# Attention probabilities transposed by VectorE in 32x32 blocks and carried to their quadrants by small transfers, in place of TensorE's transposes

## The reference

```python
xn = _layernorm(x, axis=-1)
x = x + _L0_attn_ref(xn, ...) + _L0_ffn_ref(xn, ...)

# attention: 16 heads of 32, windows of W = 64 rows
qkv = xw @ qkv_w + qkv_b
attn = jnp.einsum('bnqhd,bnkhd->bnhqk', q, k) * scale
attn = attn + _rel_pos_bias(rel_bias, W)[None, None]
attn = jax.nn.softmax(attn, axis=-1)
out = jnp.einsum('bnhqk,bnkhd->bnqhd', attn, v)
return out @ proj_w + proj_b

# experts: each of 8 takes the 1024 rows with its highest scores
scores = (x_flat @ Wg.T).T
top_vals, token_idx = jax.lax.top_k(scores, capacity)
h = silu(xg @ W1.T) * (xg @ W3.T)        # per expert, written shorter here
y = (h @ W2.T) * softmax(top_vals)
out = zeros.at[token_idx].add(y)
```

## Time and profile before

| | |
|---|---|
| median of 3 runs | 2057.91 us (2055.49 to 2058.67) |
| the profiled execution | 2061.68 us |
| its span, first to last instruction | 2059.9 us |
| granted TensorE clock, mean | 0.991 |
| TensorE busy | 1999.6 us (97%) |
| VectorE busy | 1157.6 us (56%) |
| ScalarE busy | 663.1 us (32%) |
| GpSimd busy | 597.2 us (29%) |
| attention block / expert block | up to 983.8 us / the rest |

### The profile page before, as it was taken

One profiled execution on the slowest core, in us unless ns is written; L12 is line 12 of the kernel. 1 busy time (PEld: TensorE's weight loads), 2 busy tenths in 40 slices (PEclk: granted clock), 3 DMA queues, 4 the chain that ended last, 5 costly groups with the idle time before them and its releaser, 6 DMA issues.

```text
span 2059.9 us, 36125 instructions
## 1 busy us (share of the span) xinstructions
PE 1999.6 (97%) x15051; PEld 1619.1 (79%) x15051; DVE 1157.6 (56%) x1748; ACT 663.1 (32%) x1015; POOL 597.2 (29%) x416
## 2 busy tenths in 40 slices
PE   6999999999999999998899999999999999999997
PEld 4777777787778788776788888888888888888886
DVE  5666677777768877676744544346344443444221
ACT  2333322323334443332433242232332333323221
POOL 1444444445444343353022021211212012111111
PEclk9999999999999999999999999999999999999999
DMA  7133334555432111212444253333532434325311
GB/s 209 68 106 100 105 109 122 146 164 167 141 91 63 55 30 42 63 63 87 159 104 111 72 134 91 65 105 87 131 79 62 124 81 107 92 66 143 62 21 21
DMA packets 152883, 198.17 MB, mean 96 GB/s; under 512 B 19376, under 2 KB 93488, under 8 KB 152752
## 3 DMA queue, kind: packets, MB, share of 16 engines
q1 hardware_dynamic: 138416, 162.77, 26.3%
q0 software_dynamic: 14336, 33.56, 9.1%
HBM read 128.13 MB, written 51.38 MB: 87 GB/s over the span
## 4 chain that ended last, share of the span: by engine, by line
PE 52%; DVE 0%; POOL 0%; ACT 0%; issue 0%; POOLq 0%
PE ps_e L59 17%; PE ps_e L61 17%; PE ps_e L60 17%; PE ps_e L157 1%; POOL out_rows L1649 0%; DVE xn L1802 0%; DVE xgt_lo L1807 0%; ACT x_res L1717 0%; DVE w_lo L1796 0%; DVE got L165 0%; POOLq L1648 0%
## 5 line engine op out<-in xcount | busy, mean ns | idle before, releaser
L59 PE MATMUL ps_e<-xgt_hi,w_hi 128*128 128x512 f32 x1024 | 404.4, 395 | 7.7 <-DVE xgt_lo L1807 7.7
L61 PE MATMUL ps_e<-xgt_hi,w_lo 128*128 128x512 f32 x1024 | 399.3, 390 | 0.0
L60 PE MATMUL ps_e<-xgt_lo,w_hi 128*128 128x512 f32 x1024 | 399.2, 390 | 0.0
L1828 DVE TENSOR_TENSOR hm<-ps_e,silu 128x512 f32<-128x512 f32 x128 | 88.4, 691 | 458.5 <-PE ps_e L61 457.7
L59 PEld LDWEIGHTS ps_e<-xgt_hi,w_hi 128*128 128x128 f32 x1024 | 192.7, 188 | 46.0 <-DVE xgt_lo L1807 8.2
L1649 POOL DMA_INDIRECT out_rows<-x_res,idx x64 | 100.6, 1572 | 432.6 <-ACT x_res L1717 418.2
L61 PEld LDWEIGHTS ps_e<-xgt_hi,w_lo 128*128 128x128 f32 x1024 | 192.8, 188 | 40.7
L505 POOL TENSOR_TENSOR pn_sb<-p_sb,s_rec 128x1024 f32<-128x1024 f32 x64 | 121.9, 1904 | 350.0 <-DVE s_rec L1186 281.5
L60 PEld LDWEIGHTS ps_e<-xgt_lo,w_hi 128*128 128x128 f32 x1024 | 192.9, 188 | 38.2
L59 PE MATMUL ps<-xt_hi,wqk_hi 128*128 128x512 f32 x512 | 215.2, 420 | 3.2 <-issue 2.3
L186 POOL DMA_INDIRECT x_in<-xn_rows,idx x64 | 74.4, 1162 | 486.8 <-DVE idx L178 308.8
(11 more groups left out here) (182 smaller groups left out, 3489.1 us busy)
## 6 DMA issues: line engine op xcount, KB each, us to landing
x_f<-in_w SPq DMA_DIRECT2D x48, 512.0 KB
raw<-in_w SPq DMA_DIRECT2D x48, 512.0 KB
x_res<-in_x SPq DMA_DIRECT2D x16, 1024.0 KB, 5.3
out_rows<-x_res SPq DMA_DIRECT2D x16, 1024.0 KB, 4.2
xn<-x_in SPq DMA_DIRECT2D x256, 64.0 KB, 2.0
xn_rows<-xt_plain SPq DMA_DIRECT2D x10, 1024.0 KB, 4.2
xn<-xn_rows SPq DMA_DIRECT2D x32, 256.0 KB, 5.3
x_in<-xn_rows SPq DMA_DIRECT2D x28, 256.0 KB, 4.6
```

Of the source, the lines that this page charges most:

```text
L59: nc.tensor.matmul(out, w_hi, x_hi, start=start, stop=False)
L60: nc.tensor.matmul(out, w_hi, x_lo, start=False, stop=False)
L61: return nc.tensor.matmul(out, w_lo, x_hi, start=False, stop=stop)
L1828: v.tensor_tensor(hm[:, m % 2, :], ps[:, 2 * (m % 2) + 1, :], silu[:, m % 2, :], ALU.mult).then_inc(hm_ready, 1)
```

## The change

TensorE's transposes and `pt_diag` go, in all groups but the last two (62 and 63). GpSimd writes `pn_sb` in halves by key. VectorE transposes it in place in 32x32 blocks, one instruction of 1024 columns (`turn_probs`). Eight transfers of 32 partitions by 2 KB then carry the blocks to the quadrants in which the product wants them, into one of two buffers `pt` (`probs_piece`, `spread_probs`): four are issued by SyncE, four by ScalarE, each from its own queue, after a wait for `pn_turned` and for the product of the group two before. GpSimd's next multiply waits until the pieces of the group before have landed (`pt_in`), and so does the product.

The product is now one of 64 keys for one window at a time: 32 matmuls of 64 columns in place of 16 of 128, into two banks. V gets a second buffer. The eight PSUM banks are dealt out anew, with V's tiles and output tiles in banks of the scores and of Q and K, so their matmuls wait for other evictions than before. The orders of all queues are rewritten: V0 and V1 stand ahead of the scores of s, V2 and V3 ahead of those of s+1, the four output tiles around those of s+2, and each of the four products directly ahead of scores, while the bias add of the last group moves into the next chunk. The output rows' stored copy is waited for later by SyncE (`load_res`). Chunk 1's normalized rows are transposed by TensorE like those of chunk 0 (`first_xt`, `first_rows`), and both chunks' rows are stored by `keep_first`, 16 transfers each. The weight units come in another order, and V's evictions of chunk 0 stand between the splits.

The core of the diff:

```diff
+        pn_sb = sb("pn_sb", [P, TT * 4 * W])
+        pt = [sb(f"pt_{i}", [P, 2, TT, 4, QD]) for i in range(2)]
...
+        SP, OT, OT2, QB, KB = 0, 4, 5, 6, 7
+        V_BANK, P_BANK, FINAL_BANK = (0, QB, 0, QB), (0, 1, QB, KB), (0, 1, 2, 3)
...
+        def probs_piece(s, w, i, j):
+
+            half = TT * 4 * QD
+            src, dst = QD * (2 * w + i), QD * (2 * w + j)
+            return pt[s % 2][dst:dst + QD, i, :, :, :].rearrange("p t h q -> p (t h q)"), pn_sb[src:src + QD, half * j:half * (j + 1)]
...
+            def spread_probs(s):
+
+                sp.wait_ge(pn_turned, s + 1)
+                if s >= 2:
+                    sp.wait_ge(o_mm, s - 1)
+                for i, j in ((0, 0), (0, 1), (1, 0), (1, 1)):
+                    dst, src = probs_piece(s, 0, i, j)
+                    sp.dma_start(dst, src).then_inc(pt_in, 16)
...
+            keep_first(0)
             keep_scores(0)
+            keep_first(1)
+            spread_probs(0)
+            spread_probs(1)
+            keep_scores(1)
+            for c in range(1, NCH):
+                s, n, j = G * c, c + 1, c + LEAD
+                if n < FAR:
                     load_x(n)
...
+                spread_probs(s - 2)
+                load_res(c - 1)
                 if FAR < j <= NCH:
                     load_back_ahead(j - 1)
+                spread_probs(s - 1)
                 if n < FAR:
                     keep_xn(n)
+                    load_back(n)
+                spread_probs(s)
...
+            def normalise(s):
                 pool.wait_ge(rec_ready, s + 1)
...
+                    if s >= 1:
+                        pool.wait_ge(pt_in, PIECES * s)
+                    nc.gpsimd.tensor_tensor(halves_first(pn_sb[:, :]), p_sb[:, :, :, :].rearrange("p t h (j c) -> p (t h) j c", c=QD),
+                                            s_rec[:, :].unsqueeze(2).unsqueeze(3).to_broadcast([P, TT * 4, 2, QD]),
+                                            ALU.mult).then_inc(norm_ready, 1)
...
             def pv(s, m):
...
+                    pe.wait_ge(pt_in, PIECES * (s + 1))
...
+                    for w in range(2):
+                        keys = slice(W * w, W * (w + 1))
+                        for h in range(4):
+                            col = HD * (4 * m + h)
+                            i = nc.tensor.matmul(ps[HD * h:HD * (h + 1), (OT, OT2)[w], W * t:W * (t + 1)],
+                                                 v_rows[keys, t, col:col + HD], pt[s % 2][keys, :, t, h, :], start=True, stop=True)
...
+            def chunk(c):
...
                 project_q(s, 0)
                 project_k(s, 0)
+                project_v(c, 0)
+                hunt(c, 1)
+                project_v(c, 1)
+                pv(s - 2, 2)
+                pe.wait_ge(v_ready, TT * c + 1)
+                slot_read(c, 1)
                 scores(s)
+
+                pe.wait_ge(v_ready, TT * c + 2)
                 project_q(s + 1, 1)
+                hunt(c, 2)
                 project_k(s + 1, 1)
                 project_v(c, 2)
+                hunt(c, 3)
                 project_v(c, 3)
...
+                pe.wait_ge(v_ready, TT * c + 4)
+                project_q(s + 2, 2)
+                project_k(s + 2, 2)
+                hunt(c, 4)
...
+                hunt(c, 5)
+                lists_of(5)
+                project_out(c - 1, 2)
+                lists_of(6)
                 pv(s, 0)
...
+            def turn_probs(s):
+                dve.wait_ge(norm_ready, s + 1)
+                blocks = pn_sb[:, :].rearrange("p (b c) -> p b c", c=QD)
+                nc.vector.transpose(blocks, blocks).then_inc(pn_turned, 1)
```

More of the change, by code:

```diff
@@ L673, in hunt_chunk, with chunk @@
                 hunt(c, 5)
                 o_hi_part(s, 0, projected=TT * c)
+                exponentials(s + 2)
                 q_part(s + 3, 3)
[L677 to L680 removed]
                 k_part(s + 3, 3)
[L682 to L684 removed]
+            def chunk(c):
                 s = G * c
[L686 to L694 removed]
+                last = c == NCH - 1
+                o_hi_part(s - 3, 1)
+                spread_probs(s - 2)
@@ L715, in chunk @@
+                o_hi_part(s - 1, 3)
+                q_part(s + 2, 2)
+                exponentials(s + 1)
+                k_part(s + 2, 2)
+                if not last:
                     xt_hi_part(c + 1)
-                    k_part(s + 2, 2)
-                o_hi_part(s, 0, projected=None if first else TT * c)
+                spread_probs(s + 1)
+                o_hi_part(s, 0, projected=TT * c)
+                exponentials(s + 2)
                 q_part(s + 3, 3)
-                probs_t_part(s + 1)
@@ L735, in _ @@
             split_hi(1)
-            first_xt_hi()
-            for u in range(2, ALL_SPLIT):
-                split_hi(u)
+            split_hi(2)
             act.wait_ge(const_in, 96)
             nc.scalar.activation(q_bias[:, :], qk_bias[:, 0:G], ACT.Copy, scale=SCALE).then_inc(q_bias_ready, 1)
-            act.wait_ge(consts, 14)
             act.wait_ge(q_bias_ready, 1)
-            chunk(0, first=True)
+            q_part(0, 0)
+            split_hi(3)
+            k_part(0, 0)
+            split_hi(4)
@@ new lines, in chunk, with lists_of @@
+            def chunk(c):
+                s, n, j = G * c, c + 1, c + LEAD
+                ahead, last = FAR < j <= NCH, c == NCH - 1
+                def lists_of(g):
+                    if last:
+                        compact(nc, pe, lists, ps[:, LISTS, :], 0, g, parts=2)
+                project_q(s, 0)
+                project_k(s, 0)
+                project_v(c, 0)
+                hunt(c, 1)
+                project_v(c, 1)
+                pv(s - 2, 2)
+                pe.wait_ge(v_ready, TT * c + 1)
+                slot_read(c, 1)
@@ L1100, in last_chunk @@
                     project_out_group(t, 3).then_inc(p_mm, 1)
-            pe.wait_ge(consts, 14)
-            first_xt()
-            chunk(0, first=True)
-            for c in range(1, NCH - 1):
+            pe.wait_ge(consts, 12)
+            first_xt(0)
+            first_chunk()
+            for c in range(1, NCH):
                 chunk(c)
-            last_chunk()
+            last_rows()
         @block.vector
@@ L1211, in layernorm_apply_ahead @@
                     dve.wait_ge(gatef_mm, j - FAR)
-                for t in range(TT):
+                for t in tiles:
                     nc.vector.tensor_scalar(by_quadrant(xt_f[:, t, :]), by_tile(x_f[:, t, :]), mv_f[:, t, 0:1], rstd_f[:, t:t + 1],
@@ L1506, in last_chunk @@
[L1506 to L1515 removed]
+                v_part(c, 2)
+                turn_probs(s)
@@ L1535, in _ @@
             split_lo(0)
-            first_xt_lo()
-            for u in range(1, V_SPLIT):
-                split_lo(u)
+            first_xt_lo(0)
+            split_lo(1)
+            split_lo(2)
+            layernorm_stats(1)
             gate_rows(0)
-            for u in range(V_SPLIT, NO_PN_RAW):
-                split_lo(u)
-            layernorm_stats(1)
+            split_lo(3)
             layernorm_apply(1)
-            for u in range(NO_PN_RAW, ALL_SPLIT):
-                split_lo(u)
             dve.wait_ge(const_in, 96)
-            dve.wait_ge(consts, 14)
-            chunk(0, first=True)
+            dve.wait_ge(consts, 12)
+            v_part(0, 0)
+            split_lo(4)
+            v_part(0, 1)
+            split_lo(5)
+            add_bias(0, 0)
+            normaliser(0)
+            v_part(0, 2)
+            turn_probs(0)
+            v_part(0, 3)
+            add_bias(1, 1)
+            split_lo(6)
+            split_lo(7)
+            normaliser(1)
+            first_xt_lo(1)
+            turn_probs(1)
+            add_bias(2, 2)
+            gate_rows(1)
+            o_lo_part(0, 0)
+            normaliser(2)
             for c in range(1, HUNT):
```

846 lines of the change are left out of this document (393 added, 453 removed).

## The result

The changed kernel takes **2084.78 us** (median of 4, 2083.11 to 2089.13) against 2058.29 for the kernel before (4 runs beside it): ratio 1.0131, 95% interval [1.0119, 1.0143], slower by 1.3%. The forecast was 2017, faster, with 2043 as its high end.

A forecast was written before the change was run, and what follows sets the result against it. TensorE, busy 97%, was taken as the bound. Gains and losses 34 - 10 + 7 + 2 + 3 + 5 = 41 us off 2061.7, less 3.8, gave 2017 us; range 1996 to 2043.

The forecast's parts named there:

- What TensorE saves: Ordinary chunk: 4 x 0.89 us of transposes and 4 x 0.17 of product saved, 3.7 after a 0.5 wait.
- Chunk 0: First chunk: two old waits go, TensorE idles 8.5 us for the first pieces; 5 us gained (0 to 9).
- The pieces of s-2, issued from 0.8 to 3.3, land at 5.3: Ordinary chunk: transfers of the group two back land 2.0 us after issue, before the multiply at 8.0 overwrites their source.
- the 1.0 us of slack of V1's eviction: Ordinary chunk: V1's eviction ends at 11.9 us, and Q of s+1 needs it at 13.0.
- T = 0: Zero of the walk through an ordinary chunk: the end of the scores of group s-1.
- the forecast's own signs of being wrong: ScalarE's four issues under 1 us or over 4, a piece landing later than 4, VectorE's transpose not about 1.3.
- the rivals on late pieces: Pieces land late behind other transfers: still faster at 2047 us (chance 0.10), or slower at 2086 (chance 0.08).
- the slower rival: Each us pieces of s-2 land after 9.0 costs 30 us over 15 chunks; 2086 us, chance 0.08.
- three of them 10 us back: Search chunks 10 to 12: each 3.4 us slower, 10 in all (bounds 6 gained, 21 lost).
- The fifth round: Search chunks: ScalarE's four issues, waiting for VectorE's transpose, stand ahead of the counts; TensorE idles 4.5 us.
- may wait 0.5 us: Gate matmuls of an ordinary chunk, at 34 us, wait up to 0.5 us for the next rows.
- Half clock was priced once, at the fifth round: Search chunks: matmuls at half clock after the 4.5 us idle, 1.7 us added a chunk.

The follow-up runs named there:

- sync_late_loads: all_sync with SyncE beginning the load of the next rows and the store of rows normalised ahead behind the pieces of s-2; 2080.1 us.
- sync_light_res: all_sync with only 256 KB of the 1 MB of residual rows loaded from chunk 5 on, work left out; one run, 2056.4 us.
- sync_store_behind: all_sync with only the 1 MB store of rows normalised ahead (chunks 5 to 9) begun behind the pieces of s-2 and the residual rows; 2064.0 us.
- all_sync: The changed kernel with all eight transfers of a group begun by SyncE, none by ScalarE; 2062.5 us, 1.0017 to the kernel before.
- v_first: The changed kernel with VectorE's evictions of V1 and V3 ahead of the transposes of probabilities and the round parts; 2092.4 us.
- sync_heavier_rounds: all_sync with VectorE making the first two comparisons of each of the 16 search rounds twice, work added; 2093.2 us.

## Why the prediction was wrong

**What TensorE saves: right.** Chunk 14 of the kernel after runs without a wait, in 52.96 us, and a plain chunk took 56.99: 4.0 off, with 4.2 forecast (chunk 14 has small matmuls of the lists in place of the gate's, of nearly the same length: 0.85 us for 1.0). The product's block is 0.78 us (358.99 to 359.77), taken at 0.91. VectorE's transpose takes 1.24 (1.29 forecast), GpSimd's multiply 1.90, four issues on ScalarE 2.7 in the search chunks (2.5 forecast).

**Chunk 0: right in mechanism, too small in size.** The pieces of group 0 wait for SyncE's stores as forecast (5.1 us, forecast 8.5), and the stage gains 12.0 instead of 5. The stores of the two chunks' rows took 10.1 us each and not 12, and began at 27.0 and not 29, so the pieces landed at 52.7 and not 59.

**The step that failed first: "The pieces of s-2, issued from 0.8 to 3.3, land at 5.3"**, and with it the 1.0 us of slack of V1's eviction. The landing of 2.0 us was a row of another part of the kernel, in which nothing else moved. In chunks 5 to 9, 2 MB of other transfers are begun just ahead. In chunk 6 the pieces land 12.6 us after T = 0 and not 5.3, and 6.9 us after the last issue; a piece later than 4 us was one of the forecast's own signs of being wrong, and so were four issues over 4 us on ScalarE, which took 4.50 here. sync_late_loads, sync_light_res and sync_store_behind show that what stands ahead does it, the 1 MB store above all. This is the place of the rivals on late pieces, and their price holds: 12.6 is 3.6 beyond the 9.0 that the forecast could bear, and TensorE waits 1.51 and 2.20. But it holds in five chunks and chunk 10, not 15, and it is paid once a chunk. The waits for V (10.8) and for pieces (3.9) and the half clock (9.5) are 24 of the 29 us by which chunks 5 to 9 miss the forecast. That the measured 2084.8 lies beside the slower rival's 2086 is chance: that sum had 69 us from this cause alone.

**The step that failed by most: the search chunks, "three of them 10 us back", measured 36.4.** The fifth round stands as forecast and costs 8.2 and not 4.5. By the trace the transpose is late because VectorE's steps run under GpSimd's instructions, 3.6 us of it; the term took their times from a quiet stretch. The two evictions come 2.1 to 2.8 and 0.9 to 1.4 us late in chunks 11 to 13 (forecast 1.5 and 0.9), and 7.8 in chunk 10, where two things come together: GpSimd's multiply waits 6.4 us for late pieces, as in chunks 5 to 9, and VectorE's terms of the ties (3.4 us) stand ahead of the eviction as well, which the forecast left out.

**The wait for the next rows at the gate, "may wait 0.5 us".** It is 1.1 to 2.4 us in each of chunks 1 to 9, 14.3 in all against 4.5, and half of the 9 us by which chunks 1 to 4 miss the forecast. In all_sync it is 4.7 in all, so the issues on ScalarE have a part in it; by which path stays open.

**Half clock was priced once, at the fifth round.** It came after other waits of over 2 us too: 24 us in chunks 1 to 12 by the split above, against 5 in the forecast.

**Causes that were priced one at a time.** ScalarE's issues (19 of 22 us through the fifth round) and VectorE's order are two causes at the same rounds: with one gone the other is next. The range had no sum of a late landing, a late round and half clock together: its worst cases were 15 us gained in chunks 1 to 9 and 21 lost in the search chunks, and 4 and 36 were lost.

What stays open: whether chunks 5 to 9 could carry the pieces in an order that was not tried, above all with the store behind the pieces of s-2 and the load that waits for it behind those of s-1; whether the store harms by its bytes or by their direction; and what the search chunks would take with GpSimd's instructions elsewhere.

## What to carry to other kernels

When work moves off the bounding engine, walk each stage with its own traffic. Here the price of a transfer was set by what was begun ahead of it, on either queue, and the price of some VectorE instructions by what GpSimd did at that moment. A stall of 2.2 us on TensorE, with one of 1.5 before it, cost 4.7 where the clock fell behind it (2.2 idle, 7.9 for a block of 5.4), so waits can cost more than their own sum. When a transfer is moved in a queue, look for the wait that belongs to it: a store put directly ahead of the load that waits for it held SyncE, and the pieces behind, for up to 10 us. A wait taken away at one place of a full engine's order comes back at the next (v_first), so test the order with added work (sync_heavier_rounds) before mending it.

## What the runs showed of the hardware

- A VectorE instruction on 128x3 elements took 1.49, 1.75 and 1.22 us instead of 0.16 when a GpSimd instruction was running, and ended 0.02 us after it; in the search ten of ten that began so did. Two comparisons of 128x512 took 2.89 instead of 0.88.
- A piece of 64 KB landed 2.0 us after its issue when no 1 MB store was begun just ahead, and 3.8 to 7.0 us when one was (sync_store_behind against all_sync, chunks 5 to 9, last piece of s-2).
- Pieces begun by ScalarE alone were as late as SyncE's behind SyncE's loads (46.6 us of waits in six places against 35.4 in five): the queue of its own gave no way past them.
- Four issues of 64 KB took 2.7 us on ScalarE in chunk 10 (DMA share of the stage 0.29) and 4.5 in chunk 6 (0.64).
- After 2.17 us (at 302.35) and 2.40 us (at 212.87) without work TensorE's matmuls came at 0.42 us instead of 0.227 for seven steps. After the waits of 1.1 to 1.9 us at the gate in chunks 1 to 9 none did.
